# A fused transformer kernel on one core: Gram-matrix row steps for the orthogonalisation, and attention in pairs of steps with four 32-row products together

## What is computed

```python
attn = softmax(einsum('bhqd,bhkd->bhqk', q, k) * hd ** -0.5)
o = einsum('bhqk,bhkd->bhqd', attn, v) ...          # three layers, two batches: six blocks
...
U, _ = jnp.linalg.qr(P)                             # P: 144 x 64
R = expm(A)                                         # A: 64 x 64, skew, one per batch
z = einsum('btn,nd->btd', x, U)
x_rot = x + einsum('btd,nd->btn', einsum('btd,bde->bte', z, R) - z, U)
```

## Time and profile before

| what | value |
|---|---|
| median of 3 runs | 1083.63 us (1082.55 to 1086.33) |
| the profiled execution | 1077.8 us, its span 1075.7 us |
| mean granted TensorE clock | 0.624 of 2.4 GHz |
| PE busy | 857.7 us (80%), 3551 matmuls |
| DVE busy | 662.4 us (62%), 2080 instructions |
| ACT busy | 385.2 us (36%) |
| POOL busy | 163.9 us (15%) |
| HBM traffic | 13 GB/s over the span |

### The profile page before, as it was taken

One profiled execution on the slowest core, in us unless ns is written; L12 is line 12 of the kernel. 1 busy time (PEld: TensorE's weight loads), 2 busy tenths in 40 slices (PEclk: granted clock), 3 DMA queues, 4 the chain that ended last, 5 costly groups with the idle time before them and its releaser, 6 DMA issues.

```text
span 1075.7 us, 11316 instructions
## 1 busy us (share of the span) xinstructions
PE 857.7 (80%) x3551; PEld 454.5 (42%) x3551; DVE 662.4 (62%) x2080; ACT 385.2 (36%) x682; POOL 163.9 (15%) x353
## 2 busy tenths in 40 slices
PE   5565889896997679799777897979886879979856
PEld 1332333333673333477444343635333544335425
DVE  4478876777537887752578667475767364674232
ACT  0311343332451433345334331325332445545412
POOL 5201013101131000223311003011002021002020
PEclk9855665555796655569865555755555775568557
DMA  3000001000021000002200000000000000000000
GB/s 100 22 1 5 17 12 43 2 16 0 21 64 32 1 0 1 1 16 56 56 0 1 1 1 15 13 1 1 1 1 1 28 1 1 0 1 1 1 11 12
DMA packets 18108, 14.95 MB, mean 14 GB/s; under 512 B 3295, under 2 KB 15479, under 8 KB 18050
## 3 DMA queue, kind: packets, MB, share of 16 engines
q1 hardware_dynamic: 18002, 14.22, 4.8%
q10 hardware_dynamic: 48, 0.02, 0.0%
HBM read 13.62 MB, written 0.61 MB: 13 GB/s over the span
## 4 chain that ended last, share of the span: by engine, by line
PE 61%; DVE 31%; issue 4%; ACT 2%; POOL 2%; DMA 0%; SPq 0%; DVEq 0%; POOLq 0%; ACTq 0%
PE m_bank L1259 11%; PE o_bank L1280 11%; DVE row_max L823 8%; PE d_bank L1399 5%; PE s_bank L1248 3%; PE m_bank L1437 3%; PE d_bank L1341 3%; PE m_bank L1267 2%; PE d_bank L1385 2%; PE d_bank L1230 2%; PE d_bank L1312 2%; DVE h_tok L882 2%; PE d_bank L1386 2%; PE d_bank L1387 2%; PE d_bank L1388 1%
## 5 line engine op out<-in xcount | busy, mean ns | idle before, releaser
L667 ACT ACTIVATE probs<-s_bank 128x512 f32<-128x512 f32 x384 | 220.4, 595 | 486.1 <-PE s_bank L1248 483.5
L823 DVE TENSOR_REDUCE row_max<-m_bank 128x1 fp32r<-128x512 f32 x384 | 256.0, 686 | 151.0 <-PE m_bank L1259 145.8
L1259 PE MATMUL m_bank<-k_t,q_t 32*128 32x512 f32 x384 | 211.8, 731 | 63.1 <-DVE q_rows L1070 24.5
L1248 PE MATMUL s_bank<-q_t,k_t 32*128 32x512 f32 x384 | 233.9, 729 | 6.2 <-ACT probs L667 5.4
L1280 PE MATMUL o_bank<-probs,v_aug 128*32 128x512 f32 x768 | 172.2, 986 | 3.9 <-DVE o_tok L841 3.2
L1259 PEld LDWEIGHTS m_bank<-k_t,q_t 32*128 32x128 f32 x384 | 79.8, 264 | 181.6 <-issue 62.7
L1248 PEld LDWEIGHTS s_bank<-q_t,k_t 32*128 32x128 f32 x384 | 88.2, 265 | 30.6 <-ACT probs L667 15.6
L593 POOL TENSOR_TENSOR h_tok<-h_tok,mod 128x144 f32<-128x144 f32 x48 | 24.0, 500 | 269.2 <-DVE h_tok L882 269.2
L1399 PE MATMUL d_bank<-w_all,g_act 128*128 128x144 f32 x480 | 61.0, 287 | 0.0
L1399 PEld LDWEIGHTS d_bank<-w_all,g_act 128*128 128x128 f32 x480 | 59.4, 190 | 2.3 <-issue 2.3
L1437 PE MATMUL m_bank<-q_rows,ident 64*64 64x144 f32 x128 | 43.9, 442 | 18.9 <-DVE q_rows L1070 18.9
(11 more groups left out here) (224 smaller groups left out, 1335.0 us busy)
## 6 DMA issues: line engine op xcount, KB each, us to landing
raw_a<-in_L_cond_w_dram SPq DMA_DIRECT2D x10, 288.0 KB
w_all<-in_L_cond_w_dram SPq DMA_DIRECT2D x10, 288.0 KB
w_rows<-in_L_cond_W_dram SPq DMA_DIRECT2D x8, 141.8 KB
raw_d<-in_L_cond_w_dram SPq DMA_DIRECT2D x30, 36.0 KB
x_tok<-in_x_dram SPq DMA_DIRECT2D x2, 288.0 KB, 4.5
raw_a<-in_L_cond_W_fc_dram SPq DMA_DIRECT2D x2, 288.0 KB
w_all<-in_L_cond_W_fc_dram SPq DMA_DIRECT2D x2, 288.0 KB
out_dram<-moe SPq DMA_DIRECT2D x4, 144.0 KB, 1.9
```

Source lines behind the costliest of these rows:

```text
L667: act.activation(probs[:, n % PROBS, :], s_banks[n % S_BANKS][:, :], ACT.Exp, scale=HD ** -0.5)\
L823: dve.tensor_reduce(row_max[:, grp % 2, t, MAXROW + 32 * j:MAXROW + 32 * j + 1], bk[:, :], AX.X, ALU.max).then_inc(drained, 1)
L1248: pe.matmul(s_banks[n % S_BANKS][:, :], k_t[rows, par, g, kt * P:(kt + 1) * P], q_t[rows, par, g, :], start=True, stop=True).then_inc(s["s ...
L1259: pe.matmul(bk[:, :], q_t[rows, par, g, t * P:(t + 1) * P], k_t[rows, par, g, :], start=True, stop=True).then_inc(s["max_full"], 1)
```

## The change

**Orthogonalisation.** `p_load` now computes the Gram matrix P^T P (64 x 64) beside P transposed, and ScalarE copies both into `aug` (64 x 208). A step `gs` j, of which there are 63, is an elimination step on aug: TensorE broadcasts row j from column j on (208 - j columns), VectorE takes the reciprocal of the pivot from PSUM, the coefficient from column j of aug, and updates aug from column j + 1 on. The copy and the two products with sums are gone.

**Attention in pairs.** The loops run over 192 pairs of steps. A pair computes two score tiles into s_pair (two banks, one tensor), then two products for maxima into m_pair (two banks, one tensor), on the four row groups. One exponential works on 128 x 1024, one reduction on 2 x 512 columns. Scores of pair p wait for the exponential of pair p - 1, maxima for the reduction of the maxima before. Of a group's 8 pairs, pair 1 has two such products for maxima, the second behind o_turn and PV, pair 7 none; `max_turn` moves to pair 7. In the first maxima, m_pair and s_pair alternate. Scores are issued before the maxima of the pair.

**Banks.** s_pair 2, m_pair 2, o_bank 1, x_bank 1, d_banks 2. The ring x of one bank carries all solver products and max_turn. Slots and solver parts of both steps run once per pair. While two parts with a bank are due in a pair, no maximum is put into the first.

```diff
-S_BANKS, M_BANKS, D_BANKS = 2, 3, 2
+D_BANKS = 2
+PAIR = 2
...
-QR_CHAIN = [("p_load",)] + [("mgs", j) for j in range(S)] + [("unit_cols",)]
+QR_CHAIN = [("p_load",)] + [("gs", j) for j in range(S - 1)] + [("unit_cols",)]
...
-MAX_SHARE = [2, 2] + [1] * (GSTEPS - 4) + [0, 0]
-TURN_AT = GSTEPS - 2
+MAX_AT = [[(0, 1)], [(1, 0), (0, 0)]] + [[divmod(p + 1, 2)] for p in range(2, GPAIRS - 1)] + [[]]
+TURN_AT = GPAIRS - 1
+def slots_of(p):
+    return SLOTS[PAIR * p] + SLOTS[PAIR * p + 1]
...
-        s_banks = [bank(f"s_bank{i}") for i in range(S_BANKS)]
+        s_pair = ctx.enter_context(nc.psum_tensor("s_pair", [P, PAIR * 512], F32))
+        m_pair = ctx.enter_context(nc.psum_tensor("m_pair", [P, PAIR * 512], F32))
-        m_banks = [bank(f"m_bank{i}") for i in range(M_BANKS)]
+        x_bank = bank("x_bank")
...
+                act.wait_ge(s["scores_full"], p + 1)
+                act.activation(probs[:, n % PROBS:n % PROBS + PAIR, :],
+                               s_pair[:, :].rearrange("p (i n) -> p i n", i=PAIR), ACT.Exp, scale=HD ** -0.5)\
...
+            def take_max(grp, t, half, pair):
                 dve.wait_ge(s["max_full"], seen.next("max_full"))
+                dve.tensor_reduce(rows[:, PAIR * half:PAIR * half + PAIR, MAXROW],
+                                  pair[:, :].rearrange("p (i n) -> p i n", i=PAIR), AX.X, ALU.max)\
+                    .then_inc(s["maxed"], 1)
...
-                elif kind == "mgs":
+                elif kind == "gs":
                     j = step[1]
-                    row = bk[0:S, 0:C]
                     dve.wait_ge(s["solver_full"], full)
-                    link(dve.tensor_copy(bc_row[:, :], row))
-                    dve.tensor_tensor_reduce(out=bc_sq[:, :], in0=bc_row[:, :], in1=bc_row[:, :], ...)
-                    dve.tensor_tensor_reduce(out=bc_scr[0:S, :], in0=q_rows[:, :], in1=bc_row[:, :], ...)
+                    dve.reciprocal(s_small[:, 1:2], bk[0:S, j:j + 1]).then_inc(s["dve_done"], 1)
                     fill[0]()
                     dve.wait_ge(s["dve_done"], done[0])
-                    link(dve.reciprocal(s_small[:, 1:2], s_small[:, 3:4]))
+                    link(dve.tensor_scalar(s_small[:, 2:3], aug[:, j:j + 1], s_small[:, 1:2], neg_after[:, j:j + 1],
                                            ALU.mult, ALU.mult))
+                    drain(dve.scalar_tensor_tensor(out=aug[:, j + 1:S + C], in0=bk[0:S, j + 1:S + C],
+                                                   scalar=s_small[:, 2:3], in1=aug[:, j + 1:S + C], ...))
...
+                    left = sum(part[0] in SOLVER_BANK for part in parts_of(p - 1))
+                    for part in parts_of(p - 1):
+                        fill[0] = fill_once if left < 2 else lambda: None
+                        solve(part)
+                        left -= part[0] in SOLVER_BANK
...
+            def scores(p):
+                if p:
+                    pe.wait_ge(s["probs_ready"], p)
+                for i in range(PAIR):
+                    rows = slice(32 * (first + i), 32 * (first + i) + 32)
+                    ins = pe.matmul(s_pair[:, 512 * i:512 * i + 512], k_t[rows, par, g, kt * P:(kt + 1) * P],
+                                    q_t[rows, par, g, :], start=True, stop=True)
+                ins.then_inc(s["scores_full"], 1)
+            def max_scores(grp, t, half, pair, depth):
+                if issued >= depth:
+                    pe.wait_ge(s["maxed"], issued + 1 - depth)
...
+                scores(p)
+                for t, half in maxima[:1]:
+                    max_scores(grp + 1, t, half, m_pair, 1)
+                if p % GPAIRS == 2 and grp > 0:
                     o_turn(grp - 1)
+                if p % 2 == 1 and p > 2:
+                    pv(p // 2 - 1)
+                for t, half in maxima[1:]:
+                    max_scores(grp + 1, t, half, m_pair, 1)
+                if p % GPAIRS == TURN_AT and grp + 1 < BLOCKS * G:
                     max_turn(grp + 1)
+                for _ in range(slots_of(p)):
                     next(woven)
+                for part in parts_of(p):
                     solver(part)
```

More of the change, by code:

```diff
@@ L643, in _ @@
             woven = side(WOVEN)
-            for n in range(BLOCKS * STEPS):
-                for _ in range(SLOTS[n]):
+            for p in range(PAIRS):
+                for _ in range(slots_of(p)):
                     next(woven)
-                for part in SOLVER_PLAN[n]:
+                for part in parts_of(p):
                     solver(part)
@@ L739, in solver @@
                 if step[0] in SOLVER_BANK:
-                    bk, drained, before = mring.take()
+                    bk, drained, before = xring.take()
                     full = seen.next("solver_full")
@@ L1167, in solve @@
             def solve(part):
-                solver(part, mring.take() if part[0] in SOLVER_BANK else None)
+                solver(part, xring.take() if part[0] in SOLVER_BANK else None)
             for slot, _ in enumerate(side(HEAD)):
@@ L1172, in _ @@
                     solve(part)
-            for i in range(T * GRP):
-                take_max(0, *divmod(i, GRP))
-                for part in first_parts(i):
+            for i in range(HALVES * T):
+                take_max(0, *divmod(i, HALVES), (m_pair, s_pair)[i % 2])
+                for part in first_parts(2 * i + 1):
                     solve(part)
@@ L1253, in max_scores @@
                 par, g = grp // G % 2, grp % G
-                rows = slice(32 * j, 32 * j + 32)
-                if grp % G == 0 and t == 0 and j == 0:
+                issued = seen.next("max_pairs") - 1
+                if issued % GPAIRS == 0 and grp % G == 0:
                     for w in stacks[grp // G]:
                         pe.wait_ge(*w)
-                bk, _ = take(mring)
-                pe.matmul(bk[:, :], q_t[rows, par, g, t * P:(t + 1) * P], k_t[rows, par, g, :],
-                          start=True, stop=True).then_inc(s["max_full"], 1)
+                if issued >= depth:
+                    pe.wait_ge(s["maxed"], issued + 1 - depth)
@@ L1262, in max_turn @@
+                for i in range(PAIR):
+                    rows = slice(32 * (PAIR * half + i), 32 * (PAIR * half + i) + 32)
+                    ins = pe.matmul(pair[:, 512 * i:512 * i + 512], q_t[rows, par, g, t * P:(t + 1) * P],
+                                    k_t[rows, par, g, :], start=True, stop=True)
+                ins.then_inc(s["max_full"], 1)
             def max_turn(grp):
-                for i in range(M_BANKS):
-                    pe.wait_ge(m_drained[i], (mring.n + M_BANKS - 1 - i) // M_BANKS)
@@ L1265, in max_turn @@
-                bk, placed[grp] = take(mring)
+                pe.wait_ge(s["maxed"], seen.n["max_pairs"])
+                bk, placed[grp] = take(xring)
                 for t in range(T):
@@ L1419, in solver @@
                     return
-                bk, ready = take(mring)
+                bk, ready = take(xring)
                 chain = 0 if step in QR_CHAIN else 1 if step in EXP_CHAIN else 2
@@ L1486, in _ @@
                     solver(part)
-            for i in range(T * GRP):
-                max_scores(0, *divmod(i, GRP))
-                for part in first_parts(i):
+            for i in range(HALVES * T):
+                max_scores(0, *divmod(i, HALVES), (m_pair, s_pair)[i % 2], 2)
+                for part in first_parts(2 * i + 1):
                     solver(part)
```

160 lines of the change are left out of this document (68 added, 92 removed).

## The result

The changed kernel takes **1109.04 us** in the median of 4 runs (1105.07 to 1110.32) against 1084.02 for the kernel before beside it: ratio 1.0223, interval 1.0189 to 1.0256, so it is slower by some 24 us. The forecast was 1098, range 1055 to 1128. The execution in the profile took 1110.29 us, its span 1108.5; that of the kernel before lay 5.8 us under its median, so the two profiles stand 33 us apart where the medians stand 25. From here on a kernel's distance to the kernel before is (ratio - 1) x 1083.6 us, since the runs were made on different chips, each beside the kernel before.

The account below looks back on a forecast made before the run. TensorE was taken to bind most stages, with some 10 to 15% lost to waits. The terms -5 - 9 + 12 + 2 + 11 + 27 - 30 + 7 = +15 us on the 1083.63 median gave 1098.6, range 1055 to 1128.

Parts of the forecast that it names:

- single solver bank (4): Where LU and the exponential share a pair, the second product waits for VectorE's drain: +11 without slots, +27 with.
- second maximum (in 2 and 5): Two maxima through the same banks in pair 1 delay later pairs; +7 over 18 groups, plus part of the attention-only groups' +12.
- row steps (1): Lighter Gram-Schmidt steps save VectorE time: -5 us in the first maxima, -9 in two VectorE-bound stages, elsewhere only a shorter chain.
- the rest of the pairs: Pairing apart from solver bank and second maximum, including TensorE's saving of 30 us in pairs with slots; -25 altogether.
- The loops (2): Attention without double buffers: an attention-only group takes 23.3 us against 19.9; four such groups near the end cost +12.
- (d): Rival: solver-bank waits at their dear end (+48) and a lower granted clock, 1135 us; chance 0.08.
- (b): Rival: TensorE arrives after VectorE has mostly drained, so the solver-bank and extra-maxima waits vanish, 1058 us; chance 0.27.
- (e): Rival: the four products do not overlap, one half running after the other, +0.4 x 192, 1175 us; chance 0.02.
- (c): Rival: gains and losses cancel, TensorE's idle time growing by what its work shrinks, 1080 to 1087 us; chance 0.11.

Follow-up runs that it names:

- side banks: Changed kernel with 27 products of the exponential taking their bank from the two d_banks instead of x_bank: 1068.46 us, ratio 0.9849.
- old loop: Kernel before, unpaired and with its old steps, given one bank for solver and turn and two for maxima: 1109.12 us, ratio 1.0282.
- even maxima: Changed kernel with one pair of maxima in each of a group's 8 pairs, instead of two in pair 1 and none in pair 7: 1078.77 us, ratio 0.9995.
- steps alone: Kernel before with only the 63 row steps on the Gram matrix; attention, banks and plan as before: 1052.76 us, ratio 0.9729.
- last kernel: Changed kernel with 27 exponential products moved to the d_banks and one pair of maxima in each pair: 1043.33 us, ratio 0.9606.

## Why the prediction was right, and where it was not

The sign held, and so did the two costs named as largest; the time lies 11 us above the forecast, and part of that closeness is luck, as the terms show:

| term | forecast | measured, known to some | from |
|---|---|---|---|
| single solver bank (4) | +38 | +41, 5 | after less side banks; old loop +31 |
| second maximum (in 2 and 5) | about +16 | +25, 6 | after less even maxima; +26 on side banks |
| row steps (1) | -14 | -29, 9 | steps alone; the same on the pairs |
| the rest of the pairs | -25 | -13, 10 | last kernel less steps alone, -42.7 + 29.4 |
| sum | +15 | +24 | |

The +16 is four attention-only groups at 23.3 - 21 (the 21 was worked out only for the run with even maxima), plus +7; the -25 is what is left of the pairs' +29 after 38 and 16. Two terms too small (3 and 9 us), one gain too large (12), one gain too small (15): the errors cancel down to 9, and that is luck. The measured column adds up to +24 by construction, since its last term is what is left over; it confirms nothing.

**The single bank (4)** was worked out from one wait in a pair without slots, and the timeline shows it nearly to the hundredth (1.30 for 1.25). For the 14 pairs with slots the value of 1.9 each was a choice between 1.25 and 3.4. The waits themselves were not at the low end: of the 26, 13 lie between 1.23 and 1.42 us (17 us in all), and the other 13 take 53 us; six of them, all in groups with slots, are longer than the 3.4 of the dear end, up to 7.38. The 70 us of waits cost only 41 because others come in their place when they go: with the side banks TensorE waits for the maxima 16.1 us instead of 9.1, and max_turn waits 10.2 us for LU where it had not waited. So the sum of this term came out right, but its waits were longer than forecast and cost less than they lasted, which is luck again.

**The row steps (1).** The step that failed is "Elsewhere it only shortens the chain, next": the gain was booked only at the start and in the two stages bound by VectorE, and at nothing in all other groups that hold these steps. Measured it is 29, in both loops. The two stages bound by VectorE did give 6.4 us in steps alone (35.6 to 32.1, 51.8 to 48.8) against the 9 booked. But all groups 0 to 7, which hold the Gram-Schmidt steps, give 20, first before, then steps alone:

```profile
87.40:425.70 338.30, 276.74 (x1084) 138.20 (x1084) 239.06 (x826) 125.08 (x220) 48.63 (x84) 0.60 0.06 17
```

```profile
80.10:398.40 318.30, 274.61 (x1084) 135.34 (x1084) 196.23 (x583) 124.83 (x220) 47.82 (x84) 0.62 0.07 18
```

TensorE works only 2 us less there; its idle time went from 61.6 to 43.7 us. So the chain of the steps had held TensorE back also where TensorE was called the bound. In the loop of pairs it is the same: from old to new steps, 7 us up to the first scores, 17 in groups 0 to 7 and less than 1 in all that follows. The 8 us that the profile of steps alone gains behind group 7 lie in the two groups at the higher clock.

Up to the first scores the steps gave 7.3 us (87.4 to 80.1 in steps alone), against the forecast 5: in after VectorE alternates one double maximum and one step every 2.07 us, not the 2.35 forecast and not the 2.98 of the earlier trace rows. The 0.15 us booked for a product that comes late is not there, and 0.07 of the reciprocal's 0.15 hides in the reduction. The chain of after in order of time (start us, us, what):

```profile
63.26 1.23 DVE row_max L832
64.48 0.08 DVE s_small L1067
64.56 0.03 issue
64.58 0.28 DVE s_small L1071
64.86 0.02 issue
64.88 0.43 DVE aug L1073
65.31 0.02 issue
65.33 1.23 DVE row_max L832
```

The stage bound by VectorE gained nothing as a whole in after (52.1 to 51.9), because the pairs took back there what the steps gave (it takes 54.6 us in pairs with the old steps).

**The loops (2).** The attention-only group came out at 23.3 exactly, with PE idle for 4.8 of it, but not by an exact working. The five terms from pair 1 to pair 3, 2.6 + 0.4 + 2.16 + 0.7 + 1.1, add up to 6.96 and not to the 6.6 that was carried on, so the group should have read 23.7; measured are 7.14 us (scores at 936.80 and 943.94), and the other pairs were a little shorter than forecast. The timeline shows how:

```profile
936.80 0.79 PE L1256 MATMUL s_pair<-q_t,k_t 32*128 32x512 f32 x2 [0.72 <-ACT probs L679]
...
937.47 0.79 PE L1271 MATMUL m_pair<-k_t,q_t 32*128 32x512 f32 x2
...
938.19 1.94 PE L1292 MATMUL o_bank<-probs,v_aug 128*32 128x512 f32 x8
938.30 1.23 DVE L832 TENSOR_REDUCE row_max<-m_pair 128x2 fp32r<-128x1024 f32 x1 [0.89 <-PE m_pair L1271]
940.05 0.79 PE L1271 MATMUL m_pair<-k_t,q_t 32*128 32x512 f32 x2
...
942.17 0.79 PE L1271 MATMUL m_pair<-k_t,q_t 32*128 32x512 f32 x2 [0.90 <-DVE row_max L832]
```

The maxima of pair 1 start at 937.47, the second at 940.05, those of the next pair at 942.17: 2.6 and 2.1, as worked out. What had not been seen is the first line with the second: the four products do not stay together. The scores go when ScalarE has read s_pair, the maxima 0.67 later when VectorE has read m_pair, and the two halves keep TensorE busy for 1.46 us where a burst of four takes 0.79. The burst of the earlier trace rows was forecast for every pair.

This does not explain why the rest of the pairs gained 13 and not 25. In the last kernel, from which the 13 is read, the four start within 0.19 us of each other in six of this group's eight pairs, as here:

```profile
885.87 0.79 PE L1273 MATMUL s_pair<-q_t,k_t 32*128 32x512 f32 x2
...
885.88 0.79 PE L1288 MATMUL m_pair<-k_t,q_t 32*128 32x512 f32 x2
```

TensorE is busy for 759.4 us in it against 851.5 with the steps alone, 92 us less where at most 77 were forecast, and yet the two spans are alike (1042.2 and 1041.5): its idle time grew from 190.0 to 282.8. So the packing gave what was forecast, and the waits took it. Among the waits that grew is that of the scores for the exponential before them (4.6 us in 11 waits, then 23.2 in 26), as the single s_pair lets one expect; which of them cost the time was not tested.

The rule of the Trainium skill that spoke against the change, TensorEngine Tiling (Array Packing), PSUM Bottleneck, that packing speeds up TensorE and not the emptying of PSUM, agrees with this stage: TensorE 18.5 us busy instead of 19.2, the group 3.4 us longer. Of these 3.4 us, 2.0 are the second maximum (the group takes 21.3 in the last kernel).

The four groups near the end, booked at +12, took 10 us more together (3.4, 5.9, -0.6 and 1.4). One of them was also hit by the clock, which only rival (d) had priced. It has a step of work beside it; first before, then after:

```profile
928.20:945.60 17.40, 16.38 (x81) 6.33 (x82) 11.19 (x19) 10.38 (x19) 1.88 (x8) 0.75 0.00 1
```

```profile
958.10:981.00 22.90, 19.52 (x84) 7.31 (x84) 10.97 (x11) 8.78 (x9) 1.88 (x8) 0.50 0.00 1
```

5.5 us instead of 3.4, at a clock that stood at 0.75 before and at 0.50 after.

**What was named as telling.** TensorE's busy total down by 50 to 70: 53. The double reduction at 1.22: 1.225. Some 23 waits for LU of over 1.2 us: the profile lists 26, all of them over 1.2. VectorE's total down by 80 to 95: wrong, 67. The row steps alone took 55.6 (662.4 to 606.8) where 63 x 0.9 was said, but the pairs took 6.7 (662.4 to 655.7), not 192 x 0.15 = 29. A likely reason, not tested by itself: the kernel before ran many of its reductions two in a row, 1.29 for both the earlier trace rows, which leaves 0.065 to save and not 0.15. TensorE's idle total grows: by 86.

**The rivals.** (b), that the waits are hidden, falls with the 70 us of waits and the 41 us that came back with the side banks. (e) falls with TensorE's total. (d) wanted a dearer bank and a lower clock: the single bank cost 41 us and not 59 (11 + 48), and the mean granted clock of the profiled executions was 0.643 after and 0.624 before, lower only in single groups. (c), that gains and losses cancel, falls with the interval, 20 to 28 us.

**What stays open.** Without the exponential, the table's other terms would put the paired kernel 29 - 25 + 13 = 17 us under the kernel before; measured it was 2.7 under, each with an interval of some 6 us. Some 14 us are not accounted for. The bank shared by the steps and the turn of the maxima is one place for them (in after, L1279 waits for the Gram-Schmidt steps); it was not tried with a bank of its own.

## What to carry to other kernels

Count PSUM banks by the dependency chains that pass through them, not by tiles in use: one bank for two chains ties them together, and TensorE, in order, holds back everything behind (here the waits of 70 us fell to 2.5, and 41 us of the time came back, when the products took other banks). Before batching instructions, look in the timeline whether they already overlap; if so the batch brings little (here some 13 us, known to 10), and its uneven remainder (two maxima in one pair) can cost more than that (25 us). When a change has two halves, measure each: here one half, worth 29 us, was hidden under the other.

## What the runs showed of the hardware

- An instruction over 1024 columns is only a little cheaper than two over 512: VectorE's row maximum 1225 ns against 2 x 686, ScalarE's exponential 1022 against 2 x 595. Two single reductions back to back took 1290, so batching saved VectorE 65 ns where they already stood together.
- Products of 32 rows in two pairs issued 0.67 us apart overlap hardly at all (each lasts 0.79, the second ended 0.67 later than the first), and two pairs 0.01 us apart overlap wholly: what is saved by row groups is decided by when the operands and banks come free.
- The granted clock of a stage differed without any change of its code: 0.61 and 0.72 for two groups in the kernel before and in that with lighter steps elsewhere, 95.7 and 86.9 us. The attention-only group with even maxima took 18.1 us at 0.78 and 21.3 at 0.50. The mean clock of the kernel before itself lay anywhere from 0.617 to 0.678, its time from 1069 to 1085 us.
